# A fused attention and mixture-of-experts layer: routing tables for 16 tiles at a time in place of 8, and one buffer for the marks of padded keys

## The reference, cut to what matters

```python
g_probs = softmax(flat @ wg.T + gb)            # 2 groups
g_idx = argmax(g_probs)
e_logits = flat @ we.T + eb                    # 8 experts
masked = where(g_idx == egid, e_logits, -inf)
p_expert = softmax(masked) * g_prob
topv, topi = top_k(p_expert, 2)
h = swiglu(flat @ w1.T)
for e in range(8):
    routed += h * w_se[:, e:e+1] @ w2[e].T
out = shared(flat) + routed                    # shared: swiglu(flat @ w_in.T) @ w_out.T
```

## Time and profile before

| | |
|---|---|
| time, median of 3 runs | 1137.24 us (1136.03 to 1137.77) |
| time of the profiled execution | 1135.77 us |
| its span, first to last instruction | 1134.1 us |
| mean granted TensorE clock | 0.978 of full speed |
| busy: PE | 1067.0 us (94%) |
| busy: DVE | 851.0 us (75%) |
| busy: POOL | 514.0 us (45%) |
| busy: ACT | 471.8 us (42%) |
| scatters L1503 on POOL | 64, together 64.7 us |

### The profile page before, as it was taken

The page is one execution under the profiler, slowest core; times in us unless marked ns, Lnnn a source line. Parts: engine busy times, 40 slices in busy tenths (PEclk is TensorE's granted clock), DMA queues, the critical chain, the costliest instruction groups (busy, mean ns, idle before and its releaser), DMA issues.

```text
span 1134.1 us, 22176 instructions
## 1 busy us (share of the span) xinstructions
PE 1067.0 (94%) x7283; PEld 901.5 (79%) x7283; DVE 851.0 (75%) x1863; ACT 471.8 (42%) x722; POOL 514.0 (45%) x613
## 2 busy tenths in 40 slices
PE   3769999999999999999999999999999999999997
PEld 2557888888788788788888877888887888888886
DVE  7768888897987887987888666557454688888886
ACT  3546556556556555565555522233221111111111
POOL 4234447448357366465373624000001566666564
PEclk8889999999999999999999999999999899999999
DMA  6795657747656665765666112687652554555451
GB/s 134 147 226 137 139 95 161 148 111 129 147 127 127 131 134 135 120 156 129 105 125 135 45 47 83 207 268 232 213 173 99 166 160 150 164 167 151 149 174 64
DMA packets 108129, 161.84 MB, mean 143 GB/s; under 512 B 29100, under 2 KB 72942, under 8 KB 108016
## 3 DMA queue, kind: packets, MB, share of 16 engines
q1 hardware_dynamic: 96244, 122.40, 46.0%
q0 software_dynamic: 11776, 38.03, 11.1%
HBM read 76.43 MB, written 52.12 MB: 113 GB/s over the span
## 4 chain that ended last, share of the span: by engine, by line
PE 80%; DVE 9%; issue 3%; DMA 3%; ACT 2%; SPq 2%; POOL 1%; POOLq 0%; ACTq 0%; DVEq 0%
PE ps L773 16%; PE ps L718 12%; PE ps L820 12%; PE ps L735 7%; PE ps L822 6%; PE ps L628 4%; PE ps L640 4%; PE ps L671 3%; PE ps L805 3%; PE ps L593 3%; PE ps L649 2%; PE ps L623 1%; PE ps L694 1%; DVE mneg L1229 1%; DMA regr<-regr 1%
## 5 line engine op out<-in xcount | busy, mean ns | idle before, releaser
L820 PE MATMUL ps<-regr,gh 128*128 x600 | 221.0, 406 | 0.1
L897 ACT ACTIVATE Pt<-ps,pbias 77x1024 f32<-77x1024 f32 x128 | 141.5, 1105 | 100.0 <-PE ps L628 98.7
L822 PE MATMUL ps<-regr,gl 128*128 x600 | 169.7, 283 | 0.0
L1419 POOL TENSOR_TENSOR gl<-gf,gh 128x512 fp32r<-128x512 f32 x64 | 82.6, 1291 | 115.8 <-ACT gh L859 115.5
L820 PEld LDWEIGHTS ps<-regr,gh 128*128 128x128 f32 x600 | 113.5, 189 | 23.8 <-issue 0.7
L987 ACT ACTIVATE gh<-ps 128x512 fp32r<-128x512 f32 x75 | 44.8, 599 | 204.9 <-PE ps L805 204.9
L1229 DVE TENSOR_REDUCE mneg<-ps 128x8 f32<-128x616 f32 x128 | 100.0, 791 | 21.7 <-PE ps L593 15.8
L822 PEld LDWEIGHTS ps<-regr,gl 128*128 128x128 f32 x600 | 113.7, 189 | 0.0
L718 PE MATMUL ps<-x2h,winh 128*128 128x512 f32 x256 | 109.8, 429 | 0.5 <-DVE OHR L1102 0.5
L718 PE MATMUL ps<-x2h,winl 128*128 128x512 f32 x256 | 102.5, 400 | 0.0
L718 PE MATMUL ps<-x2l,winh 128*128 128x512 f32 x256 | 102.2, 399 | 0.0
(11 more groups left out here) (208 smaller groups left out, 2702.5 us busy)
## 6 DMA issues: line engine op xcount, KB each, us to landing
regr<-regr SPq DMA_DIRECT2D x96, 256.0 KB, 5.9
y_dram<-Pt SPq DMA_DIRECT2D x64, 256.0 KB, 2.1
regf<-in_x SPq DMA_DIRECT2D x32, 256.0 KB, 2.9
x<-in_x SPq DMA_DIRECT2D x32, 256.0 KB, 3.8
y_dram<-res SPq DMA_DIRECT2D x32, 256.0 KB, 2.4
regr<-regr SPq DMA_DIRECT2D x96, 77.0 KB, 5.9
x_dram<-x2h SPq DMA_DIRECT2D x14, 512.0 KB, 3.0
x_dram<-x2l SPq DMA_DIRECT2D x14, 512.0 KB, 3.8
```

The lines of the kernel that those rows point to most:

```text
L820: e.matmul(o, gh2[:, k % 3, fc, :], w2v[:, bass.ds(val, 1), fc, :, :].rearrange("p o h d -> p (o h) d"), start=fc == 0, stop=False, skip_g ...
L822: m = e.matmul(o[:, 0, :], gl2[:, k % 3, fc, :], w2v[:, bass.ds(val, 1), fc, 0, :].rearrange("p o d -> p (o d)"), start=False, stop=fc == ...
L897: e.activation(Pt[0:K, 4 * k:4 * k + 4, :].rearrange("k (n j) t -> k n (j t)", n=2), bank_of["sc", b, k][0:K, :, :], ACT.Exp, bias=pbias[: ...
L1419: e.tensor_tensor(gl[:, fc, :], gf[:, n % 2, :], gh[:, fc, :].bitcast(F), ALU.subtract).then_inc(s["gl"], 1)
```

## The change

The first 48 tiles are routed in three routes of 16 tiles in place of six of 8; tiles 48 to 63 keep their routes of 8, 4 and 4. Before, the routes were (first tile, tiles, chunk) (0,8,1), (8,8,3), (16,8,5), (24,8,7), (32,8,9), (40,8,11), (48,8,13), (56,4,14), (60,4,15). Now they are (0,16,3), (16,16,7), (32,16,11), (48,8,13), (56,4,14), (60,4,15). All tiles that a route uses are made twice as long. To make room in SBUF, `pk` loses its second half (its load now waits for the pick of the pair before), and `nti`, used once at the end of the routes, moves into `lgT`.

```diff
-ROUTES = [(4 * c - 4, 8, c) for c in range(1, NCH - 2, 2)] + [(4 * c, 4, c) for c in (NCH - 2, NCH - 1)]
+ROUTES = [(4 * c - 12, 16, c) for c in range(3, NCH - 4, 4)] + [(4 * NCH - 16, 8, NCH - 3)] + [(4 * c, 4, c) for c in (NCH - 2, NCH - 1)]
...
-        pk = sb("pk", [P, 2, G, 2, K])
+        pk = sb("pk", [P, G, 2, K])
...
-        cmp = sb("cmp", [P, 16, 4, 4])
+        cmp = sb("cmp", [P, 32, 4, 4])
...
-        OH = sb("OH", [P, 8, NC], BF)
-        OHR = sb("OHR", [P, 8, NC])
-        rec = sb("rec", [P, 8, 4])
-        slot = sb("slot", [P, 8], I32)
+        OH = sb("OH", [P, 16, NC], BF)
+        OHR = sb("OHR", [P, 16, NC])
+        rec = sb("rec", [P, 16, 4])
+        slot = sb("slot", [P, 16], I32)
+        nti = lgT[0:NC, 0:2 * P].bitcast(I32).rearrange("c (n p) -> c n p", n=2)
...
                     e.wait_ge(s["tabw"], 32)
-                    if b >= 2:
-                        e.wait_ge(s["pick"], 3 * (b - 1))
-                    e.dma_start(pk[:, h, :, :, :].rearrange("p g n k -> p (g n k)"),
+                    e.wait_ge(s["pick"], 3 * b)
+                    e.dma_start(pk[:, :, :, :].rearrange("p g n k -> p (g n k)"),
...
-                T, a0 = 2 * J, t0 % 16
+                T, a0 = 2 * J, t0 % 32
...
-                        v = dst[:, 4 * (c % 4):4 * (c % 4) + 4, :]
+                        v = dst[:, 4 * (c % 8):4 * (c % 8) + 4, :]
```

More of the change, by code:

```diff
@@ L347, in build @@
         gl = sb("gl", [P, 4, 512], R)
-        LGg = sb("LGg", [P, 16, 2])
-        LGe = sb("LGe", [P, 16, 8])
+        LGg = sb("LGg", [P, 32, 2])
+        LGe = sb("LGe", [P, 32, 8])
         upb = sb("upb", [P, P], BF)
         io = sb("io", [P, 64])
[L352 to L357, removed]
-        cmp = sb("cmp", [P, 16, 4, 4])
-        rs4 = sb("rs4", [P, 16, 4])
-        cs4 = sb("cs4", [P, 16, 4])
-        cl = sb("cl", [P, 8])
+        gm = sb("gm", [P, 16, 2])
+        dd = sb("dd", [P, 16])
+        ng = sb("ng", [P, 16])
+        mx4 = sb("mx4", [P, 32])
+        e8 = sb("e8", [P, 32, 4])
+        s8 = sb("s8", [P, 32, 4])
+        cmp = sb("cmp", [P, 32, 4, 4])
+        rs4 = sb("rs4", [P, 32, 4])
+        cs4 = sb("cs4", [P, 32, 4])
+        cl = sb("cl", [P, 16])
         ct = sb("ct", [P, NC])
-        Zt = sb("Zt", [P, 16])
-        crow = sb("crow", [1, 8 * NC], BF)
+        Zt = sb("Zt", [P, 32])
+        crow = sb("crow", [1, 16 * NC], BF)
         kint = sb("kint", [P, 1], I32)
         kcol = sb("kcol", [P, 1])
-        nti = sb("nti", [NC, 2, P], I32)
         ntb = sb("ntb", [NC, P], BF)
@@ L371, in build @@
         tk = sb("tk", [P, 6])
[L372 to L375 removed]
+        OH = sb("OH", [P, 16, NC], BF)
[3 more added lines that the diff above has]
+        nti = lgT[0:NC, 0:2 * P].bitcast(I32).rearrange("c (n p) -> c n p", n=2)
         stage = Pt[:, :, :].rearrange("p h s -> p (h s)")
[L378 removed]
+        pre = OHR[:, 0:8, :].rearrange("p a c -> p (a c)")
         gff = gf[:, :, :].rearrange("p a n -> p (a n)")
@@ L1174, in vector @@
                     e.tensor_scalar(pbias[:, :], mkT[:, :], 1.0, NEGB, ALU.is_equal, ALU.mult).then_inc(s["dcon"], 1)
-                    e.tensor_scalar(crow[:, :].rearrange("p (j c) -> p j c", c=NC), io12[0:1, :].unsqueeze(1).broadcast_to([1, 8, NC]),
+                    e.tensor_scalar(crow[:, :].rearrange("p (j c) -> p j c", c=NC), io12[0:1, :].unsqueeze(1).broadcast_to([1, 16, NC]),
                                     -1.0, float(NT), ALU.add, ALU.mult).then_inc(s["dcon"], 1)
@@ L1183, in vector @@
                     e.wait_ge(s["mk"], 16)
-                    e.tensor_scalar(pk[:, 0, :, 0, :], mk0, 1.0, None, ALU.is_equal).then_inc(s["mark"], 1)
+                    e.tensor_scalar(pk[:, :, 0, :], mk0, 1.0, None, ALU.is_equal).then_inc(s["mark"], 1)
                     e.wait_ge(s["mark"], 1)
                     e.wait_ge(s["gcon"], GCON["ramp"])
-                    e.scalar_tensor_tensor(kone[:, :, 0, :], pk[:, 0, :, 0, :], -1000.0, ramp.unsqueeze(1).broadcast_to([P, G, K]),
+                    e.scalar_tensor_tensor(kone[:, :, 0, :], pk[:, :, 0, :], -1000.0, ramp.unsqueeze(1).broadcast_to([P, G, K]),
                                            ALU.mult, ALU.add).then_inc(s["mark"], 1)
@@ L1191, in vector @@
                     e.wait_ge(s["mark"], 3)
-                    e.tensor_tensor(pk[:, 0, :, 1, :], kone[:, :, 0, :], best[:, :].unsqueeze(2).broadcast_to([P, G, K]),
+                    e.tensor_tensor(pk[:, :, 1, :], kone[:, :, 0, :], best[:, :].unsqueeze(2).broadcast_to([P, G, K]),
                                     ALU.is_equal).then_inc(s["mark"], 1)
@@ L1208, in vector @@
                     v = kf[:, :, :].rearrange("p (g c) k -> p g c k", g=G)
-                    e.tensor_tensor(kone[:, :, :, :], v, pk[:, h, :, 1, :].unsqueeze(2).broadcast_to([P, G, 2, K]),
+                    e.tensor_tensor(kone[:, :, :, :], v, pk[:, :, 1, :].unsqueeze(2).broadcast_to([P, G, 2, K]),
                                     ALU.mult).then_inc(s["pick"], 1)
@@ L1213, in vector @@
                     e.wait_ge(s["pick"], 3 * b + 2)
-                    e.copy_predicated(v, pk[:, h, :, 0, :].bitcast(I32).unsqueeze(2).broadcast_to([P, G, 2, K]),
+                    e.copy_predicated(v, pk[:, :, 0, :].bitcast(I32).unsqueeze(2).broadcast_to([P, G, 2, K]),
                                       kfirst[:, :, :].unsqueeze(3).broadcast_to([P, G, 2, K])).then_inc(s["pick"], 1)
```

## The result

| | before | after |
|---|---|---|
| median | 1136.86 us (1136.03 to 1137.77, 5 runs) | 1155.88 us (1153.24 to 1156.52, 5 runs) |
| profiled execution, its span | 1135.77, 1134.1 us | 1154.34, 1152.6 us |
| first to last transposition of the logits (L703, L702 after) | 590.75 us | 611.26 us |

The ratio is 1.0167, 95% interval 1.0155 to 1.0179: slower by 19.0 us, inside the range.

What follows compares the result with a forecast made beforehand. TensorE, 80% of the span, was taken as the bound. Terms -11.0 + 4 + 20 + 4 = +17 us on the median 1137.24 gave 1154.5 us; all low ends gave 1144, and the range ends at 1167.

Steps and rivals of the forecast that it cites:

- What goes: Three of six route starts before tile 48 disappear, shortening their chunks on TensorE: 11.0 us gained.
- What grows at the starts: Three remaining starts: longer operations on `cmp` 1.5 us, rank 1.5, rest of the route 1; 4 us lost.
- Sixteen scatters in a row: GpSimd's queue delays the `gl` of part 3; TensorE stalls 6.7 us per merged route, 20 us lost.
- The clock: Each TensorE stall brings a fall of the granted clock, 1.4 us three times: 4 us lost.
- What costs nothing: Single `pk`, `nti` in `lgT` and the longer `rec` memset: waits covered, no time lost.
- Rival A: GpSimd, busy only 45%, absorbs the scatter backlog without a TensorE stall: faster, 1130 us; chance 0.08.
- rival B: Displaced GpSimd operations block VectorE, row maxima come late, clock stays low longer: 5 us more per route, 1169.5; chance 0.06.
- Rival C: Overlooked slack hides most of TensorE's wait, 2 us per route left, no clock fall: 1136 us; chance 0.06.

Runs made afterwards that it cites:

- the kernel held back and caught up: Kernel before, all-pairs comparison two pieces later in the first six routes, delay made up before the rank so scatters keep their places: 1123.87 us, ratio 0.9901.
- the kernel with the comparison held back as well: Kernel after, each merged route's second eight scatters delayed to k = 18 on, all-pairs comparison delayed two pieces: 1153.91 us, ratio 1.0087.

## Why the prediction was right, by its own steps

- **What goes**: forecast -11.0, measured -10.4. The difference is the plain chunk, 38.26 us now against 38.02 with eight scatters in it. Chunks without scatters cost 0.25 us more, which I had no row for: before, every chunk had either a start or scatters.
- **What grows at the starts**: forecast +0.5 for the blocked pair, measured 2.28 - 1.76 = 0.52. The comparison took 1.71 us in place of 1.44, not 2.9, 0.27 more, as much as its partner on `cmp` that nothing blocks (L1056 0.68, L1057 0.41), so the reading that a block doesn't grow with the blocked operation was right, and with it the section of the Trainium skill that the prediction named (SBUF — State Buffer, "Who interferes with whom"). One premise was misread: the 0.284 us of the earlier trace rows are for 128 elements, and the same operation on its 256 takes 0.41 when nothing blocks it (see the kernel held back and caught up), so it did not end by "just its unblocked time" behind GpSimd's. The rank took 234.72 to 235.85, 1.13 us in place of 0.53, so +0.60 against +0.5; of the two ways to count it, that by columns (+0.65) came nearer. A start chunk grew by 1.34 against a forecast of 1.3. The second idle time of 0.68 us I had not foreseen; since the chunk grew by no more than 1.34, part of it was made up for, and where is not shown. The part came to +6.2 in place of 4, since scatter and plain chunks grew by 0.5 and 0.25.
- **Sixteen scatters in a row**: 6.7 each, 20 in sum, against 7.1, 6.7, 6.8 and 20.6. The place, both waits and the releaser were as named; `gl` came at 292.3 on the clock of before, forecast 291.8. VectorE's wait was 7.1 us and not 5.7: I counted it from the old start of L1258, which itself came behind 0.60 us of idle time, and the `bias` came 0.8 us later than forecast (L1257 starts at 287.04, 290.07 on the clock of before, against 289.3). It ended 2.3 us ahead of TensorE's.
- **The clock**: this is the term that was mis-sized. Forecast 1.4 each from a fall beside an idle time of 1.76 us; the stalls bring falls twice as long (6.8 us against 3.4), and what their chunks lost beyond the idle time is (27.1 - 20.6) / 3 = 2.2 each, 6.5 in place of 4. In the first of them TensorE works for 4.5 us at half the clock, which by itself makes an estimated 2.25. And the two falls at starts that stayed vanished, -2.4, which no term had. These two differences, +2.5 and -2.4, nearly cancel, and that is luck: it leaves the sum as near as it is.
- **What costs nothing**: confirmed alone, ratio 0.9996.

Sum of the terms: +17 forecast, +18.5 by the spans, +19.0 by the medians. Rival A was wrong at its point of decision: GpSimd's share of 45% has nothing to do with it. But it was right that eight scatters can be absorbed, one chunk later. Of rival B one part came true, the clock stayed low for longer; a block or a late row maximum on top of the stalls is not in the trace. Rival C found nothing in it.

## What to carry to other kernels

A cheap instruction on an engine that works in order costs what it pushes past the next deadline: here 1.2 to 1.3 us for every scatter ahead of the `gl`, and next to nothing for the same scatter in eight places of the chunk behind, though behind another start of the route chunks with scatters in the same places took 0.2 to 1.2 us more. Before batching work to save a fixed price, look at what that price is: here about half of it came from one operation blocked by another engine (the six starts cost 3.9 us each with the falls of the clock, and 1.9 once the block was gone), and moving it by two places, with the work behind it kept in its old places, gave 1% where merging lost 1.7%. When a piece is moved, see that what follows it doesn't move along.

## What the runs showed of the hardware

- A VectorE operation with two SBUF inputs can be shut out over several GpSimd operations in a row: L1155, 0.47 us at its shortest, took 4.01 under three back-to-back operations of GpSimd, and in the kernel with the comparison held back as well 4.20 and 3.27; each time it ended 0.35 us behind the last of them. The lock that the Trainium skill describes (SBUF — State Buffer, "Who interferes with whom") is held for an instruction; in these three cases it was not handed over between them. In the usual case it was: L1154 ended 0.34 us behind the `bias`, and the `keys` that followed it took 1.46 us in place of 1.22.
- A scatter need not shut such an operation out: in the kernel after, L1153 runs from 254.28 wholly inside a scatter and takes 0.47 us, and in all six scatter chunks of the kernel before L1154 takes 0.47 beside one. So scatters can keep `keys` and `bias` away from it. Against it stands the kernel with the scatters spread out, where L1156 began as far behind the start of a scatter (256.73), took 2.40 us and ended 0.35 us behind the `keys` that followed the scatter.
- Whether more scatters can make a chunk faster is not shown. With eight, a chunk took 38.02 us before and 38.52 after, L1154 or L1153 at 0.47 in both; with the second eight in the next chunk it took 38.31, and the operation met `keys` again and took 1.58; with none it took 38.26. Why the scatter chunks of the kernel before are 0.24 us shorter than a chunk without scatters stays open.
- A stall of 7 us brought a fall of the granted clock of 6.8 us each time, begun while TensorE still stood; 2.3, 1.9 and 1.6 us of it lie in the idle time. Idle times of 1.76 to 2.28 us brought one of about 3.4 us in some starts and none in others: three of six before, none of three after, two of three with the second eight in the next chunk. Where these idle times were gone (held back, with or without the catching up) no start had a fall.
